# Softplus sum of a Mamba front end: from a VectorE addition to an accumulating GpSimd transfer

## The reference, cut to what matters

```
h = relu(adj @ layernorm(x) @ gcn_w + gcn_b); h = layernorm(h) * ln_g + ln_b
xz = h @ w_in;  u = silu(causal_conv4(xz[:, :256]) + conv_b);  z = xz[:, 256:]
dbc = u @ w_xp                                   # 8 columns for dt, 16 for B, 16 for C
dt = softplus(dbc[:, :8] @ w_dt + b_dt)
state[n] = exp(dt * A) * state[n - 1] + dt * B[n] * u[n]     # 16 states per channel
y = (sum over states of state[n] * C[n] + u * D) * silu(z);  x = x + y @ w_out
x = x + prob * expert(layernorm(x))              # router and experts
```

## Time and profile before

| | us |
|---|---|
| median of 3 runs | 1755.98 |
| lowest, highest | 1751.51, 1758.42 |
| profiled execution, its own time | 1760.01 |
| span of the profile | 1758.2 |
| DVE busy | 1537.9 |
| PE busy | 1434.7 |
| ACT busy | 883.6 |
| POOL busy | 790.0 |

### The profile page before, as it was taken

The page is one execution under the profiler, slowest core; times in us unless marked ns, Lnnn a source line. Parts: engine busy times, 40 slices in busy tenths (PEclk is TensorE's granted clock), DMA queues, the critical chain, the costliest instruction groups (busy, mean ns, idle before and its releaser), DMA issues. The chain is left out here.

```text
span 1758.2 us, 15991 instructions
## 1 busy us (share of the span) xinstructions
PE 1434.7 (82%) x4051; PEld 658.9 (37%) x4051; DVE 1537.9 (87%) x2022; ACT 883.6 (50%) x1574; POOL 790.0 (45%) x396
## 2 busy tenths in 40 slices
PE   5998898888889898988989888889898894523487
PEld 2433333333334444444443434444444332221354
DVE  8057969898999999999999999999999999999842
ACT  3143445363636547473827465554737383734441
POOL 0013333443435355555545545555555454545622
PEclk9999999999999998999999999999899996665699
DMA  8888899899998888888888888878888884424350
GB/s 308 280 287 289 318 336 323 315 338 363 329 350 301 296 298 298 299 302 293 289 290 296 280 303 288 301 278 304 303 298 287 286 297 164 142 90 147 108 160 16
DMA packets 157806, 476.92 MB, mean 271 GB/s; under 512 B 19693, under 2 KB 41760, under 8 KB 157586
## 3 DMA queue, kind: packets, MB, share of 16 engines
q1 hardware_dynamic: 114098, 324.56, 52.9%
q10 hardware_dynamic: 38560, 139.48, 23.0%
q0 software_dynamic: 5056, 11.87, 1.8%
HBM read 445.75 MB, written 32.97 MB: 272 GB/s over the span
## 5 line engine op out<-in xcount | busy, mean ns | idle before, releaser
L1197 PE MATMUL ps_adj<-ring,nodes 128*128 128x512 f32 x2048 | 969.5, 621 | 117.1 <-DMA ring<-adj 58.5
L506 POOL TENSOR_TENSOR h_c<-hidden,bc_ring 128x1024 f32<-128x1024 f32 x256 | 602.1, 2352 | 876.4 <-DVE inject L1057 676.5
L984 DVE TENSOR_TENSOR_SCAN hidden<-decay,state,inject 128x512 f32<-128x512 f32 x512 | 627.6, 1267 | 53.8 <-ACT decay L584 30.8
L1197 PEld LDWEIGHTS ps_adj<-ring,nodes 128*128 128x128 f32 x2048 | 396.0, 199 | 642.4 <-issue 462.4
L584 ACT ACTIVATE decay<-dt_sb,negA 128x512 f32<-128x512 f32 x512 | 339.5, 712 | 9.5 <-DVE dt_sb L1011 7.5
L1057 DVE TENSOR_TENSOR inject<-dtu_sb,bc_ring 128x1024 f32<-128x1024 f32 x256 | 314.3, 1228 | 26.5 <-DMA bc_ring<-bc_dram 21.9
L577 ACT COPY state<-hidden 128x2 f32<-128x2 f32 x255 | 49.1, 193 | 496.0 <-DVE hidden L984 495.5
L1027 DVE TENSOR_TENSOR y_sum<-y_sum,h_c 128x1024 f32<-128x1024 f32 x224 | 273.6, 1221 | 7.7 <-POOL h_c L506 4.6
L480 POOL DMA_INDIRECT out<-o_sb,out_at x68 | 98.8, 1453 | 78.5 <-DVE o_sb L887 64.4
L475 POOL DMA_INDIRECT bins<-rec,dest x60 | 87.8, 1464 | 10.2 <-issue 9.3
L1124 PE MATMUL ps_f<-u_sb,wxp_sb 128*128 128x512 f32 x64 | 44.0, 825 | 42.4 <-ACT u_sb L663 42.4
(11 more groups left out here) (203 smaller groups left out, 1271.1 us busy)
## 6 DMA issues: line engine op xcount, KB each, us to landing
ring<-adj SPq DMA_DIRECT2D x512, 512.0 KB, 5.9
bc_ring<-bc_dram ACTq DMA_DIRECT2D x256, 512.0 KB, 6.1
wd_ring<-wd_rows SPq DMA_DIRECT2D x64, 288.0 KB, 3.2
bins<-nodes SPq DMA_DIRECT2D x32, 516.0 KB, 8.0
got<-bins SPq DMA_DIRECT2D x60, 129.0 KB, 2.5
nodes<-x_rows ACTq DMA_DIRECT2D x8, 512.0 KB, 12.7
x_tile<-x_rows SPq DMA_DIRECT2D x16, 256.0 KB, 7.6
wd_rows<-Wd SPq DMA_DIRECT2D x8, 256.0 KB, 7.2
```

The lines of the kernel that those rows point to most:

```text
L506: nc.gpsimd.tensor_tensor(h_c[:, s % 2], hidden[:, s % 2], over_halves(bc_ring[:, s % BC_RING, 1]), ALU.mult).then_inc(hc_ready, 1)
L984: scan = nc.vector.tensor_tensor_scan(hidden[:, s % 2, h], decay[:, s % 2, h], inject[:, h], state[:, h, s:s + 1], ALU.mult, ALU.add)
L1197: last = nc.tensor.matmul(ps_adj[:, 0], nodes[:, m], ring[:, g % RING, m % GROUP], start=(m == 0), stop=(m == J - 1))
```

## The change: what it does, and the diff

In `body` of GpSimd, ahead of `h_c` of slot `f[13]`, a transfer from SBUF to SBUF is issued that reads `soft` and adds it onto `dt_sb` while it writes (128 partitions with 1024 float32 each, 512 KB). It waits for the same two semaphores as the addition did. VectorE's addition is gone. Since a transfer counts a semaphore up by 16, the three waits on `dt_ready` (ACT, DVE, PE) now count in sixteens.

```
-            sem("dt_ready"), sem("dtu_ready"))
+            sem("dt_ready", 16), sem("dtu_ready"))
...
                 q = 1 - p
                 fast = ffn and not front
+                f = FRONT.get(i, range(SLOTS))
                 for s in range(SLOTS):
+                    if front and s == f[13]:
+                        c.wait(soft_ready, 1, 2)
+                        c.wait(relu_ready, 1, 2)
+                        nc.gpsimd.dma_start(dt_sb[:, q], soft[:], accum_op=ALU.add).then_inc(dt_ready, 16)
...
-                        c.wait(dt_ready, d, 1)
+                        c.wait(dt_ready, d, 16)
...
-                    if front and s == f[13]:
-                        c.wait(soft_ready, 1, 2)
-                        c.wait(relu_ready, 1, 2)
-                        nc.vector.tensor_tensor(dt_sb[:, q], dt_sb[:, q], soft[:], ALU.add).then_inc(dt_ready, 1)
...
-                        c.wait(dt_ready, 1, 1)
+                        c.wait(dt_ready, 1, 16)
```

## The result

The changed kernel takes 1762.9 us (median of 20 runs, 1757.45 to 1775.01). The kernel before, on the same chips, takes 1754.94 (20 runs, 1751.03 to 1761.6). The ratio is 1.0048, 95% interval 1.0034 to 1.0063: 8.4 us more, where the forecast was 5.2 more (1761).

The account below looks back on a forecast made before the run. The adjacency stream bounds stages up to about 512 us, DVE's scan chain the rest. DMA load +4.7, stage 4 -1.1 and POOL +1.6 sum to +5.2 us: 1761 on the median's scale, own range 1753 to 1768, 8-in-10 range 1748 to 1786.

Parts of the forecast that it names:

- The issue on POOL: Issuing the new transfer takes POOL 0.98 us, as a scatter does back to back; bounds 1.99 and down to nothing.
- The dear issue: Rival: POOL's issue takes 1.99 us, `h_c` 1.0 later still in ten stages, +10 us, 1771; chance 0.18.
- the free one: Rival: POOL's issue nearly free, ten late stages and stage 4 keep their 1.14 us, -12.5, 1743.5; chance 0.10.
- POOL in ten late stages: Stages 5 to 14: transfer behind a scatter delays `h_c`, the saved 1.14 us plus 0.16 is lost; +1.6 us in all.
- E: Point in a late stage where `h_c` of slot 12 ends; times are given after it.
- Stage 4: -1.1 us: Stage 4 alone wins 1.1 us, with a gap on POOL and no adjacency wait after it.
- The landing: Transfer lands 8 us after the issue (bounds 3 and 12.2), hidden in stages 1 to 14.
- The late landing: Rival: landing takes 12.2 us, DVE waits at `dtu_sb` in stages 4 to 14; +26 on the forecast, 1787; chance 0.22.
- Stages -1 and 0: Readers held some 5 and 7 to 8 us fit into the adjacency waits of 7.78 and 9.97 us: cost nothing.
- The signs that the prediction named: Among them: early DVE waits shrink by about what is saved; ACT's `ps_adj` copies in stages 0, 3, 4 come 1 to 3 us later.
- The load in stages 2 and 3: Each transfer takes 1.6 us of all DMA engines, delaying the adjacency product; charged in stages -1, 2 and 3, +4.7 together.
- The expected gain: Dropping 16 additions wins DVE at most 16 x 1.14 = 18 us; five are taken up by early adjacency waits.

Follow-up runs that it names:

- early_dve: Changed kernel with VectorE's addition back in stages -1 and 0, the 14 other transfers kept; 1.0003 of the kernel before.
- late_slot12: Changed kernel with VectorE's addition back in stages -1 to 3, the eleven other transfers issued one slot earlier, ahead of `h_c` of slot 12; 0.9954, 1744.95 us.
- slot12: Changed kernel with all 16 transfers, from stage 1 on issued one slot earlier, ahead of `h_c` of slot 12; 0.9998 of the kernel before, 1755.42 us.
- Plain: Changed kernel with its sixteen transfers copying without the addition, one operand read instead of two; 0.9975 of the kernel before, 1749.76 us.
- the two holds: Kernel before, readers of the first two sums also waiting for 8-column transfers: three in a row per stage (1.0142, 1779.2 us) or one (1.0019).
- hold_short: Kernel before, with readers of the first two sums also waiting for one 8-column transfer in each of stages -1 and 0; 1.0019.
- the load alone: Kernel before, plus a same-size accumulating transfer onto unused rows in stages -1 and 0 that no reader of the sums waits for; 1.0020.

## Why the prediction was right, and which term was off

**The issue on POOL: right.** Taken as 0.98 from the scatter with POOL to itself, measured 0.985. The dear issue (1.99) and the free one are both out. That the new transfer does not wait for a VectorE instruction with two SBUF inputs holds: in stage 1 it runs beside `y_sum`, and still takes 0.86 us (timeline of the changed kernel):

```profile
303.52 0.86 POOL L493 DMA_DIRECT2D dt_sb<-soft  x1
303.61 1.22 DVE L1028 TENSOR_TENSOR y_sum<-y_sum,h_c 128x1024 f32<-128x1024 f32 x1
```

The Trainium skill, page "SBUF — State Buffer", section "Who interferes with whom", says that a VectorE instruction with two SBUF inputs contends with a GpSimd instruction that reads SBUF, and not with one that only writes it. The trace agrees, as the prediction applied the rule: the scatter that starts beside a `y_sum` in stage 13 takes 1.98 us, the transfer that starts beside one in stage 1 takes 0.86.

**POOL in ten late stages: the mechanism right, the 0.16 us too dear by half a microsecond.** The waits of `y_sum` for `h_c` rose from 4.6 us in 3 instances to 11.1 in 14, as foretold. But `h_c` started at E + 2.75, not E + 3.59 to 3.73: I had put a gap of 0.30 between two issues and 0.16 to 0.30 behind the second, taken from scatters, while the transfer follows the scatter without one, and `h_c` starts before the transfer's record ends. So DVE wins 0.34 us up to the next `y_sum` instead of losing 0.16. It does not keep them: the nine stages take as long as before, and early_dve is at 1.0003. Nine times 0.34 is 3.1 us, and the nine stages have 3.0 us more of waiting for `bc_ring`, a price of the late load that the prediction put at nothing. It is likely and not shown: these waits are 9.3 to 11.2 us in four of the five kernels with accumulating transfers there and 7.3 in the fifth (late_slot12), 6.4 with plain ones, and 5.0 to 7.8 in the six with additions.

That the issue in that place eats most of the saving is shown by slot12: it moves the issues of stages 1 to 14 by one slot and nothing else, the waits for `h_c` in the nine stages all but go, and 8.8 us come back. Plain points the same way, but its load is halved too. The rival that ACT, held for the landing, delays DVE is ruled out in the nine stages: there DVE's scans have no wait for ACT's `decay` in the changed kernel's trace.

**Stage 4: -1.1 us is not seen.** It lies within the spread of single profiles, and no run was made for it.

**The landing: right where it mattered.** Taken as 8, measured 9.2 (at most 10.8, in stage -1; 4.7 to 10.1 in stages 1 to 14). Counted the same way, from the start of the issue, the limits were 11.1 to 11.3. In stages 1 to 14 DVE never waits for it. One slot earlier, in slot12 and late_slot12, it takes 10.6 and 11.1 us (medians) and up to 12.5, but there the reader is a slot further off and does not wait either. The late landing (12.2) did not come in the changed kernel, though its premise did: two sources double the load (1.3 to 2.7 us), as the section "The bandwidth ceiling: the fold count and why AG ≠ RS ≠ AR" of the Trainium skill's page "Collectives: The Full Stack" has it. But the time to landing is only in small part the moving of these bytes: in stage -1 a transfer of 4 KB lands after 8.5 and 9.1 us (the two holds), 512 KB with one source after 9.1 and with two after 10.5 to 12.0; in stage 0 the three are 4.7 and 5.0, 6.4, and 6.0 to 9.0.

**Stages -1 and 0: the step that failed.** The prediction held of these holds of 5 and 7 to 8 us: "Both fit into the waits that follow, 7.78 and 9.97: nothing", and charged only the load, three times 1.6. The runs show: the whole loss goes with these two transfers (the table's two rows), about 6 us; the load of one is 2.7 us, not 1.6; and holding the readers costs about as much as the load (hold_short, with `dtu_sb` 10.7 and 6.4 us late where the changed kernel has it 9.4 and 13.0 late). The holds were taken as 5 and 8 us and came out at 9.4 and 13.0 (the 13.0 holds what stage 0 had already lost). But that they were longer is not what failed, since 7.98 and 1.92 us of the covers are left over. What failed is that the end of the cover was taken as fixed. It is the arrival of the adjacency product, and that came later: ACT's copy in stage 0 at 156.62 instead of 149.67 in the changed kernel, at 152.13 with the hold alone and 152.98 with the load alone. The load takes DMA time from the stream at once; the hold makes ACT fetch the next B and C later, where they take it (the queues' rows above). The signs that the prediction named say the same: the copies in stages 0, 3 and 4 were to be late by 1 to 3 us and are late by 7 to 9 in this profile, which is of a long run. The load in stages 2 and 3, for which +3.2 was charged, isn't resolved: 0.2% at most.

The total came out near partly by luck, because these two cost 6 us where 1.6 had been charged, while the other fourteen, charged with 3.2 - 1.1 + 1.6 = 3.7, cost 0 to 3.5 (0.03 and 0.20% in the table).

**The expected gain.** 16 x 1.14 = 18 us at the most. Five of the sixteen are waited away early, ten are lost, mostly to POOL's second issue, and the first two transfers cost 6 more. Moving the ten by one slot brings back half to most of theirs: 4.8, 7.0 and 8.7 us over nine stages in three kernels.

## What to carry to other kernels

Ahead of moving an instruction to an idle queue, look at what that engine has to start next and when: here 0.98 us on an engine that was 45% busy took more than half of a gain of 1.14 us, and the same issue one slot earlier, where its engine had a gap, took next to none of it. A transfer that nobody waits for still costs where the DMA engines set the pace, and an accumulating one counted twice here (2.7 against 1.3 us). A late reader is not free because a longer wait follows it: what is queued behind it, here the fetch of B and C, moves too, and with it the end of that wait.

## What the runs showed of the hardware that I had not expected

The issue of a transfer on POOL grows with its sources: 0.59 us for 128 rows with one, 0.985 with two, of the same bytes written. Bytes hardly matter to it: the tiny transfers of hold_short take 1.43 and 1.23 us to issue for 4 KB, where 512 KB with two sources take 1.10 and 0.90 in the same two places. They have twice the pieces (two rows of 16 bytes on each partition; 272 packets where the large one has 144), so a time that grows with pieces and sources is in line with all three, but no run varied the pieces alone. The time to landing follows the size little under full load, and the place more: the same 512 KB with two sources landed after 10.8 us in stage -1 and 4.7 in stage 14 of the changed kernel.
